# Routed expert blocks: transposes gathered behind one down product, expert numbers loaded earlier

## The chip, the cores and the metric

The kernel runs on one core of a Trainium2 chip. The metric is the device time of one execution in microseconds (us), median of several runs. The engines are TensorE (PE; PEld is its weight load), VectorE (DVE), ScalarE (ACT), GpSimd (POOL) and SyncE (SP, which issues most transfers).

## The reference

A cross-attention layer and a mixture-of-experts layer, each added to its input. The changed part is the second layer on 2048 tokens of 512 values, with 7 routed experts of which each token uses 2, and one shared expert:

```python
x = x + xattn(layernorm(x), ctx)
t = layernorm(x)                                    # 2048 x 512
gate = t @ Wr + br                                  # 7 experts, the best 2 are taken
probs = softmax(gate of the chosen 2)
u = t @ Wup[e] + bup[e]                             # 512 x 512 each
g = silu(u @ Wgate[e] + bgate[e]) * u
eo = g @ Wdown[e] + bdown[e]
x = x + sum over e of probs * eo  +  shared expert(t)
```

## The kernel before

The program has five stages on the same core: projections, attention, `output` (attention's output product, routing, the shared expert for the first half of the tokens), `routed` (the experts) and `late` (the shared expert for the second half, and the sum of all). Each stage ends at a barrier of all engines.

`output` gives each (token, expert) pair a row in `xs_dram`, in order of experts, each expert's rows filled up to a multiple of 128. `routed` then works through N = `NBLK` = 38 blocks of 128 such rows; `blk_k` holds the expert of each block (1 to 7) and `blk_w` the place of its weights. All weights are kept as a high and a low 16-bit part in `w_exp`, 7 places of one expert each; POOL loads and splits the experts from the third one on while blocks run (L192, L202 to L210). A product of a block with a 512 x 512 weight is 12 matmuls of 512 columns: 4 chunks of the contraction, for each high x high, low x high and high x low (`product`, L1907).

A block n goes through this chain:

- x: PE turns the block's rows, four 128 x 128 transposes (`transposes`, L1897, into `psX`); ACT copies out the high part `e_xT` (`hi_part`, L1834), DVE makes the low part (`lo_part`, L1862).
- u: PE's up product into `psU`; DVE scales and adds the bias (`biased`, L1865) into `e_u`; PE turns it (into `psUT`); ACT and DVE make the two parts of `e_uT`.
- g: PE's gate product into `psG`; DVE adds the bias (`e_g`), ACT takes silu (L1855), DVE multiplies by `e_u` (L1889); PE turns the result (into `psGT`); ACT and DVE make the two parts of `e_gT`.
- y: PE's down product into `psY`; ACT scales it out (`e_y`, L1848); SP stores it.

PSUM tiles `psX`, `psU`, `psUT` and `psG` are parts of one allocation, shown as `quad` in rows; `e_uT` has one buffer, `e_xT` and `e_gT` have two. The blocks are pipelined by hand: in `step(n)`, each engine does its parts of blocks n+1 (x), n (u and gate), n-1 (turning g) and n-2 (down), in the order in which the code stands; engines meet through semaphores alone. PE's order in a step is: up product of n; first half of the down product of n-2 (6 matmuls); turn g of n-1; turn u of n; second half of the down product; turn x of n+1; gate product of n. `run` writes out 4 steps, then a loop of 8 rounds with 4 steps each, then the last steps. The expert of a block is read from `blk_k` and `blk_w` into registers of PE by `value_load` (TENSOR_LOAD in an order of instructions): two loads ahead of each up product and one ahead of each down product. The addresses of the weights are set in registers between matmuls (ISA and REGISTER_ALU).

Of the kernel before, what the change touches and what calls it, by code (L numbers as in the profile page):

```python
# [21 lines left out]
F32 = mybir.dt.float32  # L22
# [36 lines left out]
UNROLL = 4  # L59
E_EARLY = 2  # L60
# [30 lines left out]
def build(nc, t, out, upto=99, dbg=None):  # L91
# [17 lines left out]
    with ctx:  # L109
# [13 lines left out]
        late_sb = Map(nc, SBUF_LO + 2 * PER_E, SBUF_LO + 3 * PER_E)  # L123
# [17 lines left out]
        blk_w = const("blk_w", [P, NBLK], I32)  # L141
# [45 lines left out]

        def load_half(eng, raw, loaded, k, half, m):

            shared = isinstance(k, int) and k in (0, E + 1)  # L190
            src = s_dram[m][:, ds(half * 2, 2), :] if shared else w_dram[m][:, ds((k - 1) * KD + half * 2, 2), :]
            eng.dma_start(raw, src).then_inc(loaded, 16)  # L192

        def split_half(pool, raw, loaded, arrived, k, half, m, n, piece):

            x = (k % E if isinstance(k, int) else k) * 2 + half
            hi, lo = (w_exp[:, ds(x, 1), m, y, :, :].rearrange("p o k n -> p (o k n)") for y in range(2))
            w = raw.rearrange("p k n -> p (k n)")
            ws = ws_tile[:, :].broadcast_to([P, KD // 2 * D])
            if piece == 0:  # L200
                pool.wait_ge(loaded, 16 * arrived)
                pool.tensor_tensor(hi, w, ws, ALU.mult).then_inc(w_scaled, 1)  # L202
            elif piece == 1:
                pool.wait_ge(w_scaled, 2 * n + 1)

                pool.tensor_tensor(seen[:, :], ws_tile[:, :], ws_tile[:, :], ALU.add)
                pool.tensor_scalar(w, w, WS, 0.0, ALU.mult, ALU.add).then_inc(w_scaled, 1)  # L207
            else:
                pool.wait_ge(w_scaled, 2 * n + 2)
                pool.tensor_tensor(lo, w, hi, ALU.subtract).then_inc(split_done, 1)  # L210

        def scale_half(act, raw, loaded, arrived, k, half, m, n, piece):

            hi = w_exp[:, k % E * 2 + half, m, 0, :, :]
# [1005 lines left out]
def output(nc, t, sem, g_):  # L1220

    w_exp, ident, oT_all, wo, slot, prob, pmat, blk_k, blk_w, b_up, b_gate = (
        g_[k] for k in "w_exp ident oT_all wo slot prob pmat blk_k blk_w b_up b_gate".split())
# [32 lines left out]
    wrap = low("wrap", [P, NBLK], F32)  # L1256
# [43 lines left out]
    with ExitStack() as ps:  # L1300
# [139 lines left out]
        def _(dve):  # L1440
# [174 lines left out]
        def _(pe):  # L1615
# [38 lines left out]
            def weight(m, y, q):  # L1654
                return w_exp[:, q // 2, m, y, q % 2, :]
# [61 lines left out]
def routed(nc, t, sem, g_):  # L1717

    w_exp, blk_k, blk_w, ident, seen, ws_tile, bias = (
        g_[k] for k in "w_exp blk_k blk_w ident seen ws_tile bias".split())  # L1720
# [22 lines left out]
    def run(eng, step):  # L1743

        peeled = 4
        left = (N - 2 - peeled) % UNROLL
        for n in range(peeled):
            step(n, n % 2, n // 2)
        if N - 2 - peeled >= UNROLL:
            with eng.Fori(0, (N - 2 - peeled) // UNROLL) as r:  # L1750
                for q in range(UNROLL):
                    step(r * UNROLL + peeled + q, q % 2, r * (UNROLL // 2) + (peeled + q) // 2)
        for n in range(N - 2 - left, N - 2):
            step(n, n % 2, n // 2)
        for n in range(N - 2, N + 2):
            step(n, n % 2, n // 2)

    with ExitStack() as ps:  # L1758
# [73 lines left out]
        def _(act):  # L1832
# [27 lines left out]
        def _(dve):  # L1860
# [6 lines left out]
            def step(n, j, i):  # L1867
                if live(n, 0):
                    dve.wait_ge(s["u_mm"], n + 1)
                    dve.wait_ge(s["b_up"], (n + 1) * 16)  # L1870
                    at_least(dve, s["g_r"], n - 1)
                    at_least(dve, s["uT_t"], n - 1)
                    biased(u[:, j], psU, 0, s["u_r"], n)
                if live(n, 1):
                    dve.wait_ge(s["gT_h"], n)
                    lo_part(gT[:, (j + 1) % 2], psGT).then_inc(s["gT_l"], 1)
                if live(n, 0):
                    dve.wait_ge(s["uT_h"], n + 1)
                    lo_part(uT, psUT).then_inc(s["uT_l"], 1)
# [14 lines left out]
        def _(pe):  # L1894
# [16 lines left out]
            def turn(n):  # L1911
                return pe.value_load(blk_k[0:1, ds(n, 1)], min_val=0, max_val=E)

            def place(n):
                return pe.value_load(blk_w[0:1, ds(n, 1)], min_val=0, max_val=E - 1)

            def step(n, j, i):
                if live(n, 0):
                    k, w = turn(n), place(n)
                    pe.wait_ge(g_["split_done"], k * (2 * NM) + 2 * NM + 1)  # L1920
                    pe.wait_ge(s["xT_l"], n + 1)
                    at_least(pe, s["u_r"], n)
                    product(psU, xT[:, j], w, 0).then_inc(s["u_mm"], 1)
                if live(n, 2):
                    w2 = place(n - 2)
                    pe.wait_ge(s["gT_l"], n - 1)
                    at_least(pe, s["y_r"], n - 2)
                    product(psY, gT[:, j], w2, 2, range(0, KD // 2))
# [18 lines left out]
            step(-1, 1, -1)  # L1947
            run(pe, step)
# [5 lines left out]
            for c, dst in enumerate((psX, psU)[:UP_EARLY]):  # L1954
                terms = [(q, x, y) for q in range(KD) for x, y in ((0, 0), (1, 0), (0, 1))]
                for i, (q, x, y) in enumerate(terms):
                    ins = pe.matmul(dst[:, :], w_exp[:, 2 + q // 2, 0, y, q % 2, c * P:(c + 1) * P], g_["xT_late"][:, 0, q, x, :],
# [4 lines left out]
def late(nc, t, sem, g_, out):  # L1962
# [28 lines left out]
    def yr(m, k):  # L1991
        return yr0[:, m, k, :] if m < 6 else yr1[:, m - 6, k, :]
# [4 lines left out]
    with ExitStack() as ps:  # L1997
# [167 lines left out]
        def _(pe):  # L2165
# [7 lines left out]
            def weight(m, y, q):  # L2173
                return w_exp[:, 2 + q // 2, m, y, q % 2, :]
# [80 lines left out]
```

## Time and profile before

| | |
|---|---|
| runs | 1024.02 us median of 3 (1016.83 to 1025.42) |
| profiled execution, first to last instruction | 1015.6 us |
| fastest run less that span | 1.2 us |
| PE busy in it | 918.0 us (90%) |
| stage `routed` | from 570 to 948 us of the span |
| PE busy from 570 to 945 us | 361.00 of 375.00 us |

The profile has no time of its own beside its span. Busy time of PE counts a matmul longer than the step from one matmul to the next, because matmuls overlap: a row of 12 begins its successor some 2.6 us after its own begin, though 2.76 us busy. So the text reads starts of rows, not busy times.

### The profile page before, as it was taken

What the parts mean: (1) busy time and instruction counts of PE and PEld (TensorE: products, weight loads), DVE (VectorE), ACT (ScalarE), POOL (GpSimd) and SP (SyncE); (2) the same over time, 40 slices, a digit from 0 to 9 for tenths busy, and PEclk for the clock granted to TensorE, in tenths of its full rate; (3) what the DMA queues carried; (4) which work ended last, traced back from release to release, by engine and by line L of the source; (5) the groups of instructions that cost most, each with busy time, mean ns of one, the idle gap of its engine ahead of it and who ended that gap; (6) DMA issues with size and microseconds to landing.
All of it is one profiled execution on the core that took longest, in us unless ns stands there. A gap on an engine that the chain in (4) does not pass through costs nothing. (4 is left out here: it accounts for less than half of the span.)

```text
span 1015.6 us, 17154 instructions
## 1 busy us (share of the span) xinstructions
PE 918.0 (90%) x5077; PEld 403.7 (40%) x5078; DVE 641.9 (63%) x1026; ACT 463.2 (46%) x846; POOL 618.7 (61%) x565
## 2 busy tenths in 40 slices
PE   3799886799989899989999599999999999999998
PEld 1354443122212122246644244454454554554443
DVE  7787777698878788367765154444444544443388
ACT  3365555688878787623351032332332332322440
POOL 5465446377777684543147589998899999000372
PEclk9899998699999999999999799999999999999999
DMA  8134435445455432143427646565555565335666
GB/s 279 32 110 141 138 105 150 135 166 176 157 174 174 149 103 66 44 126 137 174 103 278 210 166 187 167 206 168 183 189 181 188 202 163 110 124 188 220 192 232
DMA packets 104521, 162.31 MB, mean 160 GB/s; under 512 B 10904, under 2 KB 53912, under 8 KB 104080
## 3 DMA queue, kind: packets, MB, share of 16 engines
q1 hardware_dynamic: 91520, 116.45, 35.0%
q0 software_dynamic: 12896, 45.10, 13.4%
q8 instruction: 30, 0.49, 0.2%
q14 instruction: 27, 0.22, 0.1%
q10 hardware_dynamic: 48, 0.05, 0.0%
HBM read 108.08 MB, written 53.48 MB: 159 GB/s over the span
## 5 line engine op out<-in xcount | busy, mean ns | idle before, releaser
L1013 ACT ACTIVATE p_t<-a_psT 128x512 f32<-128x512 f32 x256 | 138.9, 595 | 47.7 <-PE a_psT L1136 46.4
L1060 DVE TENSOR_REDUCE nm<-quad 128x4 bf16<-128x1984 f32 x60 | 133.9, 2232 | 35.8 <-PE quad L1121 35.8
L1907 PE MATMUL quad<-w_exp,e_xT 128*128 x456 | 106.8, 385 | 7.8 <-issue 4.0
L963 POOL TENSOR_TENSOR p_sum<-p_t,p_t 128x512 f32<-128x512 f32 x64 | 81.1, 1277 | 50.1 <-ACT p_t L1013 49.8
L1907 PE MATMUL e_psY<-w_exp,e_gT 128*128 x456 | 110.7, 379 | 0.9 <-ACT e_y L1848 0.9
L1907 PE MATMUL quad<-w_exp,e_uT 128*128 x456 | 104.9, 380 | 2.5 <-DVE e_uT L1862 2.5
L1136 PE MATMUL a_psT<-q_stk,k_stk 98*128 98x512 f16 x256 | 84.9, 402 | 14.1 <-ACT p_t L1013 8.8
L210 POOL TENSOR_TENSOR w_exp<-e_raw,w_exp 128x1024 f32 (+1 forms) x42 | 91.5, 2180 | 6.0 <-POOL e_raw L207 4.5
L202 POOL TENSOR_TENSOR w_exp<-e_raw,ws_tile 128x1024 f32 (+1 forms) x42 | 80.2, 1910 | 5.1 <-DMA e_raw<-in_L_ffn_Wup_dram 4.2
L1834 ACT ACTIVATE e_gT<-e_psGT 128x512 f16<-128x512 f32 x38 | 22.7, 597 | 124.0 <-PE e_psGT L1897 124.0
L1855 ACT ACTIVATE e_g<-e_g 128x512 f32<-128x512 f32 x38 | 23.9, 630 | 107.1 <-DVE e_g L1865 107.1
L1907 PEld LDWEIGHTS quad<-w_exp,e_xT 128*128 128x128 f16 x456 | 42.0, 99 | 72.2 <-issue 28.4
L1143 PE MATMUL a_psO<-p_t,v_all 128*32 128x512 f32 x512 | 67.0, 620 | 0.0
L1907 PEld LDWEIGHTS quad<-w_exp,e_uT 128*128 128x128 f16 x456 | 41.5, 98 | 54.6 <-issue 9.9
L1907 PEld LDWEIGHTS e_psY<-w_exp,e_gT 128*128 128x128 f16 x456 | 44.5, 98 | 46.6 <-issue 1.4
L1862 DVE TENSOR_TENSOR e_gT<-e_psGT,e_gT 128x512 f16<-128x512 f32 x38 | 26.3, 692 | 54.5 <-ACT e_gT L1834 54.5
L1865 DVE SCALAR_TENSOR_TENSOR e_g<-quad,bias 128x512 f32<-128x512 f32 x38 | 26.3, 692 | 53.0 <-PE quad L1907 53.0
L1889 DVE TENSOR_TENSOR e_g<-e_g,e_u 128x512 f32<-128x512 f32 x38 | 40.5, 1066 | 26.4 <-ACT e_g L1855 26.4
L1382 POOL DMA_INDIRECT xs_dram<-xn,slot x32 | 31.7, 991 | 40.3 <-DVE slot L1562 30.2
L1136 PEld LDWEIGHTS a_psT<-q_stk,k_stk 98*128 98x128 f16 x256 | 17.9, 97 | 95.4 <-issue 55.2
L1862 DVE TENSOR_TENSOR e_xT<-quad,e_xT 128x512 f16<-128x512 f32 x38 | 26.3, 691 | 42.2 <-ACT e_xT L1834 42.2
L2037 POOL MEMSET low<- 24x1 f32 x1 | 0.1, 88 | 83.8 <-POOLq L1758 83.8
(333 smaller groups left out, 1855.0 us busy)
## 6 DMA issues: line engine op xcount, KB each, us to landing
xs_dram<-zero SPq DMA_DIRECT2D x38, 256.0 KB, 7.2
e_x<-xs_dram SPq DMA_DIRECT2D x38, 256.0 KB, 4.0
bias<-in_L_ffn_bup_dram SPq DMA_DIRECT2D x38, 256.0 KB, 3.7
bias<-in_L_ffn_bgate_dram SPq DMA_DIRECT2D x38, 256.0 KB, 3.7
ys_dram<-e_y SPq DMA_DIRECT2D x38, 256.0 KB, 3.8
q_dram<-q_st SPq DMA_DIRECT2D x24, 256.0 KB, 2.8
k_dram<-k_st SPq DMA_DIRECT2D x24, 256.0 KB, 3.7
q_stk<-q_dram SPq DMA_DIRECT2D x64, 96.0 KB
```

Source lines behind the costliest of these rows:

```text
L202: pool.tensor_tensor(hi, w, ws, ALU.mult).then_inc(w_scaled, 1)
L210: pool.tensor_tensor(lo, w, hi, ALU.subtract).then_inc(split_done, 1)
L963: pool.tensor_tensor(p_sum[:, w % SUMS, :], probs(w, 0), probs(w, 1), ALU.add).then_inc(s["sum_1"], 1)
L1013: act.activation(probs(w, k), psT[:, k % 2], ACT.Exp, scale=SCALE / (QS * QS)).then_inc(s["exp"], 1)
L1060: dve.tensor_reduce(nm[:, i, :, 0:1].rearrange("p h o -> p (h o)"), psS[:, :, 0:NMAIN], AX.X, ALU.max, negate=True)
L1136: pe.matmul(psT[:, k % 2], k_stk[0:KR, w % SLOTS, k * P:(k + 1) * P], q_stk[0:KR, w % SLOTS, :], start=True, stop=True).then_inc(s["t_mm"], 1)
L1143: ins = pe.matmul(dst[j * HD:(j + 1) * HD, :], stationary(n), moving(n), start=first, stop=last, tile_position=(0, j * HD))
L1382: pool.indirect_dma_start(g_["xs_dram"], bass.IndirectOffsetOnAxis(ap=slot[:, k, n:n + 1], axis=0), xn2[:, n, :], None).then_inc(landed, 16)
L1862: return dve.tensor_tensor(pair[:, 1], src[:, :].rearrange("p (k n) -> p k n", n=P), pair[:, 0], ALU.subtract)
L1865: return dve.scalar_tensor_tensor(dst, src[:, :], 1.0 / WS, bias[:, m, :], ALU.mult, ALU.add).then_inc(done, 1)
L1889: dve.tensor_tensor(g[:, :], g[:, :], u[:, j], ALU.mult).then_inc(s["g_r"], 1)
L1907: ins = pe.matmul(dst[:, :], stationary, moving, start=(k == 0 and chunks[0] == 0), stop=(k == len(terms) - 1 and chunks[-1] == KD - 1))
```

## The change

On PE, a step now runs: the whole down product of n-2 (12 matmuls), turn u of n, turn g of n-1, turn x of n+1, gate product of n, up product of n+1. Around the cycle of steps the products stay in the same order (gate, up, down); the second half of the down product moves ahead of the transposes, and u is turned ahead of g. ACT and DVE make the parts of `e_uT` ahead of those of `e_gT`. Only `blk_k` is loaded, and each load serves the up, gate and down product of its block as far as the code of one round reaches: 7 loads in a round of four steps where there were 12. The load for the next up product stands behind the transposes of x, ahead of the gate product. `blk_w` is gone, and with it the three DVE instructions in `output` that made it. The weights of expert k now lie at place k-1; those of the shared expert lie at place 1 in `output` and at place 0 in `late`, whose tables are laid out to match.

```diff
+        def place_of(k):
+            return {0: 1, E + 1: 0}.get(k, k - 1) if isinstance(k, int) else k - 1
...
-            link(dve.tensor_scalar(wrap[:, :], blk_f[:, :], float(E), None, ALU.is_ge))
-            link(dve.scalar_tensor_tensor(wrap[:, :], wrap[:, :], -float(E), blk_f[:, :], ALU.mult, ALU.add))
             link(dve.tensor_copy(blk_k[:, :], blk_f[:, :]))
-            link(dve.tensor_copy(blk_w[:, :], wrap[:, :]))
...
@@ -1834,14 +1833,14 @@
             def step(n, j, i):
+                if live(n, 0):
+                    act.wait_ge(s["uT_t"], n + 1)
+                    at_least(act, s["g_mm"], n)
+                    hi_part(uT[:, 0], psUT).then_inc(s["uT_h"], 1)
                 if live(n, 1):
                     act.wait_ge(s["gT_t"], n)
                     at_least(act, s["y_mm"], n - 2)
                     hi_part(gT[:, (j + 1) % 2, 0], psGT).then_inc(s["gT_h"], 1)
-                if live(n, 0):
-                    act.wait_ge(s["uT_t"], n + 1)
-                    at_least(act, s["g_mm"], n)
-                    hi_part(uT[:, 0], psUT).then_inc(s["uT_h"], 1)
...
@@ -1871,12 +1870,12 @@
+                if live(n, 0):
+                    dve.wait_ge(s["uT_h"], n + 1)
+                    lo_part(uT, psUT).then_inc(s["uT_l"], 1)
                 if live(n, 1):
                     dve.wait_ge(s["gT_h"], n)
                     lo_part(gT[:, (j + 1) % 2], psGT).then_inc(s["gT_l"], 1)
-                if live(n, 0):
-                    dve.wait_ge(s["uT_h"], n + 1)
-                    lo_part(uT, psUT).then_inc(s["uT_l"], 1)
...
@@ -1908,44 +1907,56 @@
...
-            def step(n, j, i):
-                if live(n, 0):
-                    k, w = turn(n), place(n)
-                    pe.wait_ge(g_["split_done"], k * (2 * NM) + 2 * NM + 1)
-                    pe.wait_ge(s["xT_l"], n + 1)
-                    at_least(pe, s["u_r"], n)
-                    product(psU, xT[:, j], w, 0).then_inc(s["u_mm"], 1)
+            expert_of = {}
+            def expert(n, at):
+                if at not in expert_of:
+                    expert_of[at] = pe.value_load(blk_k[0:1, ds(n, 1)], min_val=1, max_val=E)
+                return expert_of[at]
+            def step(n, at, i):
+                j = at % 2
                 if live(n, 2):
-                    w2 = place(n - 2)
+                    w2 = expert(n - 2, at - 2) - 1
                     pe.wait_ge(s["gT_l"], n - 1)
                     at_least(pe, s["y_r"], n - 2)
-                    product(psY, gT[:, j], w2, 2, range(0, KD // 2))
+                    product(psY, gT[:, j], w2, 2).then_inc(s["y_mm"], 1)
+                if live(n, 0):
+                    pe.wait_ge(s["u_r"], n + 1)
+                    at_least(pe, s["uT_l"], n)
+                    transposes(psUT, u[:, j], s["uT_t"])
                 if live(n, 1):
                     pe.wait_ge(s["g_r"], n)
                     at_least(pe, s["gT_l"], n - 1)
                     transposes(psGT, g, s["gT_t"])
                 if live(n, 0):
-                    pe.wait_ge(s["u_r"], n + 1)
-                    at_least(pe, s["uT_l"], n)
-                    transposes(psUT, u[:, j], s["uT_t"])
-                if live(n, 2):
-                    product(psY, gT[:, j], w2, 2, range(KD // 2, KD)).then_inc(s["y_mm"], 1)
+                    w = expert(n, at) - 1
                 if live(n, -1):
                     pe.wait_ge(x_ld[(j + 1) % 2], (i + 1 if j == 0 else i + 2) * 16)
                     at_least(pe, s["xT_l"], n + 1)
                     transposes(psX, x_in[:, (j + 1) % 2], s["xT_t"])
+                    after = expert(n + 1, at + 1)
                 if live(n, 0):
                     pe.wait_ge(s["uT_l"], n + 1)
                     at_least(pe, s["g_in"], n)
                     product(psG, uT, w, 1).then_inc(s["g_mm"], 1)
+                if live(n, -1):
+                    pe.wait_ge(g_["split_done"], after * (2 * NM) + 2 * NM + 1)
+                    pe.wait_ge(s["xT_l"], n + 2)
+                    at_least(pe, s["u_r"], n + 1)
+                    product(psU, xT[:, (j + 1) % 2], after - 1, 0).then_inc(s["u_mm"], 1)
...
-    low = Map(nc, SBUF_LO, SBUF_LO + g_["PER_E"])
-    yr0 = low("l_yr0", [P, 6, TOP, D], F32)
-    yr1 = sb("l_yr1", [P, NT - 6, TOP, D], F32)
+    rows_back = sb("l_rows_back", [P, NT, TOP, D], F32)
```

PE, a step in the loop, before: from the end of the first half of the down product (`e_psY`) over the transposes (`ident` with `e_g`, `e_u`, `e_x`) to the gate product (`e_uT`).

```order
L1907 MATMUL e_psY<-w_exp,e_gT 128x512
L1897 MATMUL e_psGT<-ident,e_g 128x128 [waits e_gT_l,e_g_r]
...
L1897 MATMUL quad<-ident,e_u 128x128 [waits e_uT_l,e_u_r]
...
L1907 MATMUL e_psY<-w_exp,e_gT 128x512 x2
...
L1897 MATMUL quad<-ident,e_x 128x128 [waits e_xT_l,e_x_loaded0]
...
L1907 ISA [waits e_g_in,e_uT_l]
L1907 MATMUL quad<-w_exp,e_uT 128x512 x2
```

The same place now.

```order
L1906 MATMUL e_psY<-w_exp,e_gT 128x512
L1896 MATMUL quad<-ident,e_u 128x128 [waits e_uT_l,e_u_r]
...
L1896 MATMUL e_psGT<-ident,e_g 128x128 [waits e_gT_l,e_g_r]
...
L1896 MATMUL quad<-ident,e_x 128x128 [waits e_xT_l,e_x_loaded0]
...
L1915 TENSOR_LOAD blk_k
...
L1906 ISA [waits e_g_in,e_uT_l]
L1906 MATMUL quad<-w_exp,e_uT 128x512 x2
```

Between turning u and the gate product's wait for `e_uT_l` stood 6 matmuls and 4 transposes; now there are 8 transposes and one load.

PE, between the gate product and the next up product (`e_xT`), before.

```order
L1907 MATMUL quad<-w_exp,e_uT 128x512
L1912 ISA
L1912 TENSOR_LOAD blk_k
L1912 ISA x2
L1915 REGISTER_ALU
L1915 TENSOR_LOAD blk_w
L1915 ISA x2
L1920 ISA
L1921 REGISTER_ALU [waits w_split_done]
L1907 ISA [waits e_u_r,e_xT_l]
L1907 MATMUL quad<-w_exp,e_xT 128x512 x2
```

The same place now.

```order
L1906 MATMUL quad<-w_exp,e_uT 128x512
L1945 ISA
L1946 REGISTER_ALU [waits w_split_done]
L1906 ISA [waits e_u_r,e_xT_l]
L1906 MATMUL quad<-w_exp,e_xT 128x512 x2
```

Both loads are gone from there; the waits stay.

ACT, a step in the loop, before.

```order
L1834 ACTIVATE e_gT<-e_psGT 128x512 [waits e_y_mm,e_gT_t]
L1834 ACTIVATE e_uT<-quad 128x512 [waits e_g_mm,e_uT_t]
L1848 ACTIVATE e_y<-e_psY 128x512 [waits e_y_stored1,e_y_mm]
L1850 REGISTER_ALU
L1834 ACTIVATE e_xT<-quad 128x512 [waits e_u_mm,e_xT_t]
L1855 ACTIVATE e_g<-e_g 128x512 [waits e_g_in]
```

The same place now.

```order
L1833 ACTIVATE e_uT<-quad 128x512 [waits e_g_mm,e_uT_t]
L1833 ACTIVATE e_gT<-e_psGT 128x512 [waits e_y_mm,e_gT_t]
L1847 ACTIVATE e_y<-e_psY 128x512 [waits e_y_stored1,e_y_mm]
L1849 REGISTER_ALU
L1833 ACTIVATE e_xT<-quad 128x512 [waits e_u_mm,e_xT_t]
L1854 ACTIVATE e_g<-e_g 128x512 [waits e_g_in]
```

`e_uT` has moved ahead of `e_gT`; the rest of the step stands as before.

## Rows read from the trace of the kernel before

**Rows 1.** Busy time by stage: PE, PEld, DVE, ACT, POOL, then clock, DMA share, GB/s.

```profile
570.00:945.00 375.00, 361.00 (x1833) 182.25 (x1834) 167.87 (x228) 106.75 (x190) 264.45 (x232) 0.99 0.52 172
```

**Rows 2.** Waits of PE from 598 to 933 us: total, times, longest.

```profile
PE quad L1907 <- issue: 4.0, 9, 0.6
```

**Rows 3.** PE's order of time in one step: start, us, instruction.

```profile
704.01 2.76 PE L1907 MATMUL quad<-w_exp,e_uT 128*128 x12
706.85 2.76 PE L1907 MATMUL quad<-w_exp,e_xT 128*128 x12
709.44 1.46 PE L1907 MATMUL e_psY<-w_exp,e_gT 128*128 x6
710.74 0.60 PE L1897 MATMUL e_psGT<-ident,e_g 128*128 128x128 f32 x4
711.18 0.60 PE L1897 MATMUL quad<-ident,e_u 128*128 128x128 f32 x4
711.61 1.46 PE L1907 MATMUL e_psY<-w_exp,e_gT 128*128 x6
712.91 0.60 PE L1897 MATMUL quad<-ident,e_x 128*128 128x128 f32 x4
713.44 0.39 PE L1907 MATMUL quad<-w_exp,e_uT 128*128 x1
```

**Rows 4.** PE's order of time where a round of the loop ends.

```profile
722.84 2.76 PE L1907 MATMUL quad<-w_exp,e_uT 128*128 x12
726.12 2.76 PE L1907 MATMUL quad<-w_exp,e_xT 128*128 x12 [0.52 <-issue]
```

**Rows 5.** PE's order of time in step 1, which has no down product.

```profile
586.94 0.66 PE L1897 MATMUL e_psGT<-ident,e_g 128*128 128x128 f32 x4 [1.09 <-DVE e_g L1889]
587.54 0.66 PE L1897 MATMUL quad<-ident,e_u 128*128 128x128 f32 x4
...
589.69 2.54 PE L1907 MATMUL quad<-w_exp,e_uT 128*128 x11 [1.06 <-DVE e_uT L1862]
```

**Rows 6.** PE's order of time in the last steps.

```profile
932.79 2.76 PE L1907 MATMUL quad<-w_exp,e_uT 128*128 x12 [0.37 <-DVE e_uT L1862]
...
937.72 0.66 PE L1897 MATMUL e_psGT<-ident,e_g 128*128 128x128 f32 x4 [0.88 <-DVE e_g L1889]
...
940.57 2.76 PE L1907 MATMUL e_psY<-w_exp,e_gT 128*128 x12 [0.90 <-ACT e_y L1848]
```

**Rows 7.** ACT and DVE in the same step and the next one.

```profile
711.38 0.60 ACT L1834 ACTIVATE e_gT<-e_psGT 128x512 f16<-128x512 f32 x1 [3.21 <-PE e_psGT L1897]
711.87 0.59 ACT L1834 ACTIVATE e_uT<-quad 128x512 f16<-128x512 f32 x1
712.01 0.69 DVE L1862 TENSOR_TENSOR e_gT<-e_psGT,e_gT 128x512 f16<-128x512 f32 x1 [1.37 <-ACT e_gT L1834]
712.61 0.68 DVE L1862 TENSOR_TENSOR e_uT<-quad,e_uT 128x512 f16<-128x512 f32 x1
...
717.62 1.90 DVE L1889 TENSOR_TENSOR e_g<-e_g,e_u 128x512 f32<-128x512 f32 x1 [0.70 <-ACT e_g L1855]
...
719.45 0.68 DVE L1865 SCALAR_TENSOR_TENSOR e_u<-quad,bias 128x512 f32<-128x512 f32 x1
```

**Rows 8.** PE's order of time in step 0.

```profile
578.16 0.67 PE L1897 MATMUL quad<-ident,e_u 128*128 128x128 f32 x4 [0.79 <-DVE e_u L1865]
...
580.32 2.76 PE L1907 MATMUL quad<-w_exp,e_uT 128*128 x12 [1.06 <-DVE e_uT L1862]
```

**Rows 9.** DVE's order of time in `output`: first and last instruction for `blk_w`.

```profile
534.38 0.32 DVE L1586 TENSOR_SCALAR wrap<-blk_f 128x38 f32<-128x38 f32 x1
...
535.18 0.18 DVE L1589 CAST blk_w<-wrap 128x38 int32<-128x38 f32 x1
```

**Rows 10.** Busy time and clock of short stretches (columns as Rows 1).

```profile
572.70:577.40 4.70, 4.66 (x12) 1.58 (x12) 0.00 (x0) 0.00 (x0) 3.47 (x4) 0.59 0.83 281
...
585.70:589.60 3.90, 1.84 (x13) 1.27 (x12) 3.12 (x5) 1.68 (x3) 3.73 (x4) 1.00 0.59 180
589.60:600.00 10.40, 10.31 (x54) 5.32 (x55) 4.25 (x7) 2.80 (x5) 9.30 (x10) 1.00 0.48 175
```

More of the change, by code:

```diff
@@ L59 @@
 UNROLL = 4
+PEELED = 4
 E_EARLY = 2
@@ L122, in build @@
         w_exp = nc.alloc_sbuf_tensor_at("w_exp", [P, 2 * E, NM, 2, KD // 2, D], F16, offset=SBUF_LO)
-        late_sb = Map(nc, SBUF_LO + 2 * PER_E, SBUF_LO + 3 * PER_E)
+        late_sb = Map(nc, SBUF_LO + PER_E, SBUF_LO + 2 * PER_E)
         xT_late = late_sb("xT_late", [P, B // 2, KD, 2, S], F16)
@@ L140, in build @@
         blk_k = const("blk_k", [P, NBLK], I32)
-        blk_w = const("blk_w", [P, NBLK], I32)
         ws_tile = const("ws_tile", [P, 1], F32)
@@ L194, in split_half @@
         def split_half(pool, raw, loaded, arrived, k, half, m, n, piece):
-            x = (k % E if isinstance(k, int) else k) * 2 + half
+            x = place_of(k) * 2 + half
             hi, lo = (w_exp[:, ds(x, 1), m, y, :, :].rearrange("p o k n -> p (o k n)") for y in range(2))
@@ L212, in scale_half @@
         def scale_half(act, raw, loaded, arrived, k, half, m, n, piece):
-            hi = w_exp[:, k % E * 2 + half, m, 0, :, :]
+            hi = w_exp[:, place_of(k) * 2 + half, m, 0, :, :]
             if piece == 0:
@@ L1220, in output @@
 def output(nc, t, sem, g_):
-    w_exp, ident, oT_all, wo, slot, prob, pmat, blk_k, blk_w, b_up, b_gate = (
-        g_[k] for k in "w_exp ident oT_all wo slot prob pmat blk_k blk_w b_up b_gate".split())
+    w_exp, ident, oT_all, wo, slot, prob, pmat, blk_k, b_up, b_gate = (
+        g_[k] for k in "w_exp ident oT_all wo slot prob pmat blk_k b_up b_gate".split())
     low = Map(nc, SBUF_LO + E_EARLY * g_["PER_E"], g_["O_AT"])
@@ L1255, in output @@
     blk_f = low("blk_f", [P, NBLK], F32)
-    wrap = low("wrap", [P, NBLK], F32)
     mid = Map(nc, g_["O_AT"], g_["V_AT"])
@@ L1654, in weight @@
             def weight(m, y, q):
-                return w_exp[:, q // 2, m, y, q % 2, :]
+                return w_exp[:, 2 + q // 2, m, y, q % 2, :]
             def product(dst, terms):
@@ L1717, in routed @@
 def routed(nc, t, sem, g_):
-    w_exp, blk_k, blk_w, ident, seen, ws_tile, bias = (
-        g_[k] for k in "w_exp blk_k blk_w ident seen ws_tile bias".split())
+    w_exp, blk_k, ident, seen, ws_tile, bias = (
+        g_[k] for k in "w_exp blk_k ident seen ws_tile bias".split())
     tag = "e_"
@@ L1743, in run @@
     def run(eng, step):
-        peeled = 4
-        left = (N - 2 - peeled) % UNROLL
-        for n in range(peeled):
+        left = (N - 2 - PEELED) % UNROLL
+        for n in range(PEELED):
             step(n, n % 2, n // 2)
-        if N - 2 - peeled >= UNROLL:
-            with eng.Fori(0, (N - 2 - peeled) // UNROLL) as r:
+        if N - 2 - PEELED >= UNROLL:
+            with eng.Fori(0, (N - 2 - PEELED) // UNROLL) as r:
                 for q in range(UNROLL):
-                    step(r * UNROLL + peeled + q, q % 2, r * (UNROLL // 2) + (peeled + q) // 2)
+                    step(r * UNROLL + PEELED + q, q % 2, r * (UNROLL // 2) + (PEELED + q) // 2)
         for n in range(N - 2 - left, N - 2):
@@ L1946, in step @@
                     product(psG, uT, w, 1).then_inc(s["g_mm"], 1)
-            step(-1, 1, -1)
-            run(pe, step)
+                if live(n, -1):
[3 more added lines that the diff above has]
+                    product(psU, xT[:, (j + 1) % 2], after - 1, 0).then_inc(s["u_mm"], 1)
+            rounds = (N - 2 - PEELED) // UNROLL
+            for n in range(-1, PEELED):
+                step(n, n, n // 2)
+            expert_of.clear()
+            with pe.Fori(0, rounds) as r:
+                for q in range(UNROLL):
+                    step(r * UNROLL + PEELED + q, q, r * (UNROLL // 2) + (PEELED + q) // 2)
+            expert_of.clear()
+            for n in range(PEELED + rounds * UNROLL, N + 2):
+                step(n, n, n // 2)
             pe.wait_ge(late_ld, 32)
@@ L1956, in _ @@
                 for i, (q, x, y) in enumerate(terms):
-                    ins = pe.matmul(dst[:, :], w_exp[:, 2 + q // 2, 0, y, q % 2, c * P:(c + 1) * P], g_["xT_late"][:, 0, q, x, :],
+                    ins = pe.matmul(dst[:, :], w_exp[:, q // 2, 0, y, q % 2, c * P:(c + 1) * P], g_["xT_late"][:, 0, q, x, :],
                                     start=(i == 0), stop=(i == len(terms) - 1))
@@ L1991, in yr @@
     def yr(m, k):
-        return yr0[:, m, k, :] if m < 6 else yr1[:, m - 6, k, :]
+        return rows_back[:, m, k, :]
     def row(m):
@@ L2173, in weight @@
             def weight(m, y, q):
-                return w_exp[:, 2 + q // 2, m, y, q % 2, :]
+                return w_exp[:, q // 2, m, y, q % 2, :]
             def product(dst, terms):
```

4 lines of the change are left out of this document (removed).

## The prediction, made before the changed kernel ran

> **What bounds the kernel now.** I read the busy times by stage first. The stage `routed` takes more than a third of the span, and PE is busy in 361 of 375 us there at a granted clock of 0.99 [rows 1], so PE's row of instructions sets the pace. The view of waits adds that PE waited for hardly anything the profile can name: 4.0 us of "issue" in 9 pieces, and no wait for POOL's weights [rows 2]. That total understates the gaps, since a matmul's modelled end lies after the start of the next one. I therefore went to the order of time and took the distances between starts.
>
> One step, from gate product to gate product, is 9.43 us [rows 3]. The up product's 12 matmuls take 709.44 - 706.85 = 2.59 us, and each half of the down product 1.30. Four transposes take 0.43 to 0.44. So the bare work of a step is 3 x 2.59 + 3 x 0.435 = 9.08 us. The other 0.35 lies in two places: 0.25 between gate and up product (706.85 - 704.01 - 2.59), where the two loads of the expert stand, and 0.10 between turning x and the gate product (713.44 - 712.91 - 0.43). Once in four steps, where a round of the loop ends, the first gap is 726.12 - 722.84 - 2.59 = 0.69 [rows 4]. From the gate product of step 1 to that of step 37 there are 36 steps in 932.79 - 589.69 = 343.10 us [rows 5, 6], 9.53 each.
>
> The second gap is the end of a chain through three engines. PE turns u; ACT and DVE make the two parts of `e_uT`; then the gate product may start. In the step shown it ends at 712.61 + 0.68 = 713.29 on DVE, and the gate product starts 0.15 later [rows 3, 7]. From the start of turning u to the gate product it is 713.44 - 711.18 = 2.26 us. The kernel before fills this time with the second half of the down product and the turning of x: 0.43 + 1.30 + 0.43 = 2.16. The chain is just covered.
>
> **The gap before the up product goes.** Both loads leave it. Of the single load that stands before the down product, no trace can be seen: up starts at 706.85, down at 709.44, exactly 12 matmuls later [rows 3]. A load fits under one product, and two do not. In the new order at most one load stands between products (before the down product, in the first two steps of a round), and the others stand behind transposes. I cost them at nothing; what hides them is the product, or the wait below, that PE is working through. At the end of a round the jump and one load now follow two products instead of one; the jump's own price is 0.69 - 0.25 = 0.44 us, so the bound for 8 rounds is 0 to 3.5 us. I take 0, because one load behind one product showed nothing. If only this part had been made, a step would be 9.08 + 0.10 and the gain some 12 us.
>
> **The cover of the chain goes too.** Ahead of the gate product PE now has, from the start of turning u, only twelve transposes: 3 x 0.435 = 1.30 us. The chain itself gets a little shorter, since ACT and DVE take u first. By the rows of g, which now stands where u will stand: start of turning to start of ACT 711.38 - 710.74 = 0.64, ACT to DVE 712.01 - 711.38 = 0.63 [rows 3, 7]; then DVE's 0.68 for `e_uT` and 0.15 to the gate product. That is 2.10 us. There are two places in the kernel before that already run in the new arrangement. In step 1, where no down product exists yet, turning u at 587.54 is followed by turning x alone, and the gate product starts at 589.69: 2.15 us, with g ahead in ACT and DVE, and the profile books 1.06 us of idle PE on `e_uT` [rows 5]. In step 0 it is 580.32 - 578.16 = 2.16 us, with nothing ahead, and 1.06 idle again [rows 8]. So the chain lies between 2.10 and 2.16; I take 2.10, from the steady step. PE will stand idle for about 2.10 - 1.30 = 0.8 us in every step.
>
> A step becomes three products and the chain: 3 x 2.59 + 2.10 = 9.87 us against 9.53, or +0.34 x 36 = +12.2 us. With 2.16 it is +14.4.
>
> **What else is late or early.** The up product's result must reach PE through DVE before u can be turned; the whole down product, 2.59 us, now covers that. Even in the step where DVE's multiplication took 1.90 us, `e_u` was ready at 719.45 + 0.68 = 720.13 [rows 7], and in the new order u would be turned three products after 713.44, at 721.2. ACT does `e_uT`, `e_gT`, `e_y` and `e_xT` at a pitch of 0.5, so DVE's part of `e_xT` ends some 3.5 us after the start of turning u; the up product that needs it starts 2.10 + 2.59 = 4.7 after. Stores and loads of SP hang on events that all come at the same places of the step or earlier, and its transfers have a step's time to land. In step 0 the turning of u of block 1 waits for DVE as before, so that step keeps its length but for 0.05. At the end, before, the last down product started 940.57 - 932.79 = 7.78 after the last gate product [rows 6]. Now the last turning of g comes at 2 x 2.59 = 5.2 after it (5 are needed for g: 937.72 - 932.79 = 4.93), and a chain of 2.1 follows: 7.3, a gain of 0.5. In `output`, the three DVE instructions that made `blk_w` span 535.18 + 0.18 - 534.38 less one that stays, some 0.8 us [rows 9]; PE has the down products of the first half ahead of what waits for DVE there, so I count 0, at most 0.8. The weights' new places change no wait: POOL loads the same experts in the same order. `late` keeps all its instructions.
>
> **Sum.** +12.2 for 36 steps, -0.5 at the end, 0 to 3.5 at the ends of rounds (0 taken): +11.7 us on the profiled execution, 1015.6 to about 1027.3 us of span. That execution is like the fastest run (1016.83, 1.2 above the span); the median of the runs is 1024.02. On the median the forecast is 1035.7, say 1036 us, slower by 1.15%. Its own bounds are +11.7 (chain 2.10, no edges) and +17.4 (chain 2.16, edges 3.5): 1036 to 1041 on the median, and 1028 where the runs fall like the fastest one before.
>
> **Rivals.** *The transposes cover the chain after all.* If the gate product followed the transposes at once, a step would fall to 9.08, 36 x 0.45 = 16 us less: 1008 us. For it speaks that 0.35 us a step of gaps do go. Against it stand the two places with 1.06 us of idle [rows 5, 8] and the chain's own links. It decides at a chain of 9.53 - 7.77 = 1.76 us; below that the change is no loss. 7%.
>
> *The chain is shorter than its rows, near that point.* ACT and DVE would have to start on u before all four transposes are through, by 0.2 us or so; nothing in the rows does that. Half the loss: 1030 us. 9%.
>
> *Loads are not hidden.* PE now reads the expert behind the transposes and ahead of the gate product's wait. If that reading came only after them and pushed the gate product back by the 0.25 that two loads cost before, it would add 36 x 0.25 = 9 us, and the ends of rounds 3.5: 1048 us. Against it: the idle 0.8 us has room for it. 8%.
>
> *The clock falls.* Each step would have 2.10 us in which PE only turns or stands. When PE had been idle before its first product, 12 matmuls took 4.66 us at a mean granted clock of 0.59, in part at the lower level of 1.2 GHz [rows 10]; once a step, that costs 4.66 - 2.76 = 1.9, 36 times 68 us: 1104 us. But between the up product's end and the gate product of step 1, 3.9 us with nothing but transposes and idle, the granted clock was 1.00, and it was 1.00 after [rows 10]. 2%.
>
> The Trainium skill, "TensorE: Matmul & The Clock Gate", Part 4 (PE-mode transpose), says that transposes do not count as activity for the clock in the way that matmuls do; by that rule the new run of twelve transposes and the idle behind it would be one stretch without credit, and the rival above would decide. The clock of 1.00 through step 1 speaks against it at this length.
>
> **How the numbers follow.** The forecast holds 74%. A difference of about 1% is what a measurement of this kernel can tell from none, as the three runs lie 0.8% apart; the forecast's +11.7 us and more is just above that, so I give it 0.56 for slower by over 1% and 0.18 for within. Slower: 0.56 + 0.08 + 0.02 = 0.66. Within 1%: 0.18 + 0.09 = 0.27. Faster: 0.07. The range from 1027 to 1043 us holds the forecast with its bounds, runs like the fastest one, and the half loss.
>
> **What would show it.** In the profile of the changed kernel the waits of PE should name `e_uT` on DVE in nearly every step, about 0.6 us each as booked (2.10 less the start of turning x at 0.87 and its 0.60), some 23 us in all, where it was one wait of 0.37. Gate to gate should be 9.87 us in every step, without the longer fourth one; up product 2.59 after the gate product; turning u to gate product 2.10. I am wrong if that last distance is near 1.3 to 1.8, or if gaps between products remain.

## The result, and the profile after

The changed kernel takes 1029.37 us (median of 4 runs, 1027.36 to 1034.02), the kernel before 1021.86 (4 runs beside them, 1016.83 to 1025.42). The ratio is 1.0101, with a 95% interval from 1.0058 to 1.0144: slower by about 1%. The profiled execution has a span of 1027.0 us; 1027.3 was forecast.

The stage `routed` shows it first. PE is busy for less time in the same 375 us, at the same granted clock; the columns are those of [rows 1].

```profile
570.00:945.00 375.00, 346.39 (x1784) 179.06 (x1783) 174.37 (x224) 100.01 (x186) 265.37 (x232) 0.99 0.51 165
```

The waits of PE from 598 to 945 us (total, times, longest) were hardly any before [rows 2]. Now there is one in every step, and it names `e_uT`:

```profile
PE quad L1906 <- DVE e_uT L1861: 22.9, 35, 0.7
```

PE's order of time in one step of the changed kernel (start, us, instruction), to be laid beside [rows 3]:

```profile
707.46 2.76 PE L1906 MATMUL quad<-w_exp,e_uT 128*128 x12 [0.63 <-DVE e_uT L1861]
710.06 2.75 PE L1906 MATMUL quad<-w_exp,e_xT 128*128 x12
712.65 2.75 PE L1906 MATMUL e_psY<-w_exp,e_gT 128*128 x12
715.24 0.60 PE L1896 MATMUL quad<-ident,e_u 128*128 128x128 f32 x4
715.68 0.60 PE L1896 MATMUL e_psGT<-ident,e_g 128*128 128x128 f32 x4
716.12 0.60 PE L1896 MATMUL quad<-ident,e_x 128*128 128x128 f32 x4
717.34 1.03 PE L1906 MATMUL quad<-w_exp,e_uT 128*128 x4 [0.62 <-DVE e_uT L1861]
```

The gap between gate and up product is gone (710.06 - 707.46 = 2.60), and up to down takes 2.59. From turning u to the next gate product it is 717.34 - 715.24 = 2.10 us, of which the transposes fill 1.30. Gate to gate is 9.88 us.

ACT and DVE in the same step show the links of those 2.10 us (compare [rows 7]):

```profile
711.65 2.11 DVE L1888 TENSOR_TENSOR e_g<-e_g,e_u 128x512 f32<-128x512 f32 x1 [0.69 <-ACT e_g L1854]
713.69 0.68 DVE L1864 SCALAR_TENSOR_TENSOR e_u<-quad,bias 128x512 f32<-128x512 f32 x1
715.88 0.60 ACT L1833 ACTIVATE e_uT<-quad 128x512 f16<-128x512 f32 x1 [4.26 <-PE quad L1896]
716.51 0.69 DVE L1861 TENSOR_TENSOR e_uT<-quad,e_uT 128x512 f16<-128x512 f32 x1 [2.15 <-ACT e_uT L1833]
```

From turning to ACT 0.64, ACT to DVE 0.63, DVE 0.69, and 0.14 to PE. `e_u` itself is ready at 713.69 + 0.68 = 714.37, 0.87 us before PE turns it, though the multiplication ahead of it took 2.11.

The first step of each round is a little longer. The order of time of PE and ACT there (compare [rows 4]):

```profile
735.00 0.60 PE L1896 MATMUL quad<-ident,e_u 128*128 128x128 f32 x4
735.72 0.60 ACT L1833 ACTIVATE e_uT<-quad 128x512 f16<-128x512 f32 x1 [4.34 <-PE quad L1896]
737.22 0.60 PE L1906 MATMUL quad<-w_exp,e_uT 128*128 x2 [0.74 <-DVE e_uT L1861]
```

ACT starts 0.72 after turning began instead of 0.64, the chain is 2.22, and the step 9.99. This adds 0.11 a round, 0.9 us over 8 rounds. The jump's old 0.44 is no longer seen. The kernel before had the later start too: from turning x to the gate product it took 0.61 us in the first step of a round (732.79 - 732.18) where it was 0.53.

Three places at the ends answer to [rows 5, 6, 8]. First PE's order of time in steps 0 and 1:

```profile
580.28 2.76 PE L1906 MATMUL quad<-w_exp,e_uT 128*128 x12 [1.06 <-DVE e_uT L1861]
...
588.57 1.68 PE L1906 MATMUL quad<-w_exp,e_uT 128*128 x7 [0.63 <-DVE e_uT L1861]
```

And in the last steps, up to the first product of `late`:

```profile
945.25 2.76 PE L1906 MATMUL quad<-w_exp,e_uT 128*128 x12 [1.06 <-DVE e_uT L1861]
...
952.54 2.76 PE L1906 MATMUL e_psY<-w_exp,e_gT 128*128 x12 [1.50 <-DVE e_gT L1861]
955.13 1.24 PE L1968 MATMUL quad<-xT_late,w_exp 128*128 128x512 f16 x5
```

Step 0 takes 588.57 - 580.28 = 8.29 us where it was 589.69 - 580.32 = 9.37. The 36 steps behind it take 945.25 - 588.57 = 356.68 where it was 343.10. From the last gate product to the last down product it is 7.29 instead of 7.78. So -1.08 + 13.58 - 0.49 = +12.0 us lie in `routed`; the span grew by 11.4, since `late` behind it came out 0.6 shorter.

### The profile page after: what moved, and what is told of

It is laid out like the page before. It is cut to its first block and busy times, and to the rows that moved or that the text cites. A ratio compares the mean times of both kernels' runs of the same rounds, so it can differ in the third digit from the quotient of the medians.

```text
span 1027.0 us, 16980 instructions
## 1 busy us (share of the span) xinstructions
PE 916.7 (89%) x5077; PEld 406.5 (40%) x5078; DVE 650.2 (63%) x1023; ACT 458.9 (45%) x846; POOL 618.6 (60%) x565
## 5 line engine op out<-in xcount | busy, mean ns | idle before, releaser
L1906 PE MATMUL e_psY<-w_exp,e_gT 128*128 x456 | 104.7, 379 | 1.5 <-DVE e_gT L1861 1.5
L1833 ACT ACTIVATE e_uT<-quad 128x512 f16<-128x512 f32 x38 | 22.7, 597 | 164.1 <-PE quad L1896 164.1
L1861 DVE TENSOR_TENSOR e_uT<-quad,e_uT 128x512 f16<-128x512 f32 x38 | 26.3, 691 | 92.9 <-ACT e_uT L1833 92.9
L1906 PEld LDWEIGHTS quad<-w_exp,e_xT 128*128 128x128 f16 x456 | 45.0, 99 | 57.2 <-issue 4.7
L1888 DVE TENSOR_TENSOR e_g<-e_g,e_u 128x512 f32<-128x512 f32 x38 | 50.7, 1335 | 26.4 <-ACT e_g L1854 26.4
L211 POOL TENSOR_SCALAR e_raw<-e_raw 128x1024 f32<-128x1024 f32 x42 | 44.6, 1061 | 3.2
```

The lines of the kernel that those rows point to most:

```text
L1888: dve.tensor_tensor(g[:, :], g[:, :], u[:, j], ALU.mult).then_inc(s["g_r"], 1)
L1906: ins = pe.matmul(dst[:, :], stationary, moving, start=(k == 0 and chunks[0] == 0), stop=(k == len(terms) - 1 and chunks[-1] == KD - 1))
```

## The experiments

Theory: the two loads cost 0.25 us a step and their removal gives it back; turning u starts a chain of 2.10 us, and what PE has to do in that time decides the step. The rivals were that the loads in their new places still cost PE time, that the run of transposes itself is what PE pays for, and that the clock makes the difference. "Gate 1 to gate 37" below is the distance between the starts of these gate products, 36 steps; it was 343.10 before and 356.68 after. The kernel before ran beside the experiments too: 11 runs with a median of 1021.43 us for e1 to e4, 11 with 1019.43 for e5 to e8. Spans that were expected are worked out from the 1027 us of the changed kernel's profile, and several were missed, because the place of step 1's gate product moves between executions: 588.57 us in the changed kernel, 592.57 in e7, 593.34 in e1, 593.48 in e3, though what is edited there acts in later steps or, in e7, is covered by the wait. So the distance from gate 1 to gate 37 is what tells the theories apart.

**e1_split_six.** The changed kernel with half of the down product put back, between turning g and turning x:

```diff
-                    product(psY, gT[:, j], w2, 2).then_inc(s["y_mm"], 1)
+                    product(psY, gT[:, j], w2, 2, range(0, 2))
...
                     transposes(psGT, g, s["gT_t"])
+                if live(n, 2):
+                    product(psY, gT[:, j], w2, 2, range(2, KD)).then_inc(s["y_mm"], 1)
```

Expected: 

> The changed kernel with 6 of the 12 matmuls of the down product put back between turning g and turning x. Theory (uncovered chain): from turning u to the gate product there are then 0.43 + 0.43 + 1.30 + 0.43 = 2.6 us of work against a chain of 2.10, the wait for e_uT goes, a step is 9.08 us, 36 steps are 29 us shorter than in the changed kernel, span about 999 us (16 below the kernel before). Rival (the loss comes from the loads or from the order of ACT and DVE): step stays near 9.88, span 1027. Rival (an interrupted product itself costs time): step between 9.3 and 9.6, span 1008 to 1018.

Measured: 1010.77 us (6 runs), ratio to the kernel before 0.990 [0.9875, 0.9926]; gate 1 to gate 37 in 333.30 us. PE's order of time in a typical step:

```profile
886.86 1.46 PE L1906 MATMUL e_psY<-w_exp,e_gT 128*128 x6
888.16 0.60 PE L1896 MATMUL quad<-ident,e_u 128*128 128x128 f32 x4
...
889.03 1.46 PE L1906 MATMUL e_psY<-w_exp,e_gT 128*128 x6
...
890.76 2.75 PE L1906 MATMUL quad<-w_exp,e_uT 128*128 x12
```

Turning u to gate product is now 2.60 us of work without a gap, no `e_uT` is waited for, and the step is the bare 9.08. That rules out the rival by which an interrupted product itself costs time, although the span of 1008.8 us lies in the range given for it and not at 999: 4.8 us of the difference lie ahead of step 1. But 333.30 over 36 is 9.26: some steps are longer, and the view of waits names another chain, for `e_u` ahead of turning u. The waits from 598 to 945 us:

```profile
PE quad L1896 <- DVE e_u L1864: 4.5, 6, 1.2
```

One such step, in order of time:

```profile
698.89 1.92 POOL L206 TENSOR_TENSOR w_exp<-e_raw,ws_tile 128x1024 f32 x1
698.99 2.38 DVE L1888 TENSOR_TENSOR e_g<-e_g,e_u 128x512 f32<-128x512 f32 x1 [0.70 <-ACT e_g L1854]
...
701.29 0.68 DVE L1864 SCALAR_TENSOR_TENSOR e_u<-quad,bias 128x512 f32<-128x512 f32 x1
...
702.03 0.66 PE L1896 MATMUL quad<-ident,e_u 128*128 128x128 f32 x4 [0.57 <-DVE e_u L1864]
```

The half product ahead of turning u covers the making of `e_u` for 1.30 us only. Where DVE's multiplication takes 2.4 us, that is not enough. So the down product has two gaps to fill, one on each side of turning u, and the change put all of it on one side.

**e2_split_three.** The same with a quarter put back (`range(0, 3)` ahead, `range(3, KD)` behind).

Expected: 

> The changed kernel with 3 of the 12 matmuls of the down product behind turning g. Theory: work from turning u to gate 1.30 + 0.65 = 1.95 us against a chain of 2.10, so 0.15 us of wait stays; a step is 7.78 - 0.65 + 2.10 = 9.23 us, span about 1004 us. Rival (something else than the cover of the chain makes the step long): 9.5 to 9.9, span 1014 to 1027.

Measured: 1008.86 us (4 runs), ratio 0.9885 [0.9847, 0.9922]; gate 1 to gate 37 in 335.85. A step in PE's order of time:

```profile
896.97 0.60 PE L1896 MATMUL quad<-ident,e_u 128*128 128x128 f32 x4
...
897.84 0.81 PE L1906 MATMUL e_psY<-w_exp,e_gT 128*128 x3
...
899.07 1.25 PE L1906 MATMUL quad<-w_exp,e_uT 128*128 x5
```

Turning u to gate product is 2.10 again: three matmuls (0.65) bring the cover to 1.95, the chain still ends last by 0.15, and the step is 9.23 = 9.08 + 0.15. The chain's length is the same at two amounts of cover, and the loss falls one for one with the cover. The waits for `e_u` are 1.0 us in 4. The span is 1008.4 where about 1004 was expected; 2.4 us of that lie ahead of step 1 (590.95 for 588.57), most of the rest in steps longer than the typical one. Between e1 and e2 the runs do not tell a difference.

**e3_loads_back.** The changed kernel with two fresh loads between gate and up product, and none behind the transposes of x:

```diff
-                    after = expert(n + 1, at + 1)
...
-                    pe.wait_ge(g_["split_done"], after * (2 * NM) + 2 * NM + 1)
+                    again = pe.value_load(blk_k[0:1, ds(n + 1, 1)], min_val=1, max_val=E)
+                    after = expert(n + 1, at + 1)
+                    pe.wait_ge(g_["split_done"], again * (2 * NM) + 2 * NM + 1)
```

Expected: 

> The changed kernel with two fresh loads of the expert's number between the gate product and the up product, as before; the load behind the transposes of x is gone. Theory (the loads opened the gap of 0.25 us): the gap is back, 0.25 us a step and 0.25 to 0.3 at the ends of rounds, which now fall elsewhere; 36 x 0.25 = 9 us, span about 1036 us. Rival (the gap came from the order of products or the wait on the weights, which are unchanged here): no gap, span 1027.

Measured: 1039.22 us (4 runs), ratio 1.0178 [1.0142, 1.0213]; gate 1 to gate 37 in 362.55, 5.87 more than the changed kernel, or 0.16 a step. The gap is back in PE's order of time, after gate's 2.6 us:

```profile
905.88 2.76 PE L1906 MATMUL quad<-w_exp,e_uT 128*128 x12 [0.74 <-DVE e_uT L1861]
908.64 2.76 PE L1906 MATMUL quad<-w_exp,e_xT 128*128 x12
```

In the steps of the loop it is 0.12 to 0.26 us wide and mostly under the 0.25 that was expected. Here both loads read one table and the place is worked out in a different way, so the old pair need not cost exactly this. That two loads between the gate and the up product cost PE time is shown. That the loads cost nothing in the changed kernel's places is shown by the typical steps of e1 and e8, which have them there and take the bare 9.08.

**e4_g_first.** The changed kernel with ACT and DVE back in the old order, the parts of `e_gT` ahead of those of `e_uT`; PE as changed:

```diff
+                if live(n, 1):
+                    act.wait_ge(s["gT_t"], n)
...
                 if live(n, 0):
                     act.wait_ge(s["uT_t"], n + 1)
...
-                if live(n, 1):
-                    act.wait_ge(s["gT_t"], n)
```

The same swap is made in DVE's code.

Expected: 

> The changed kernel with ACT and DVE making e_gT ahead of e_uT, while PE still turns u ahead of g. Theory (the chain through ACT and DVE sets the gate product): e_uT must wait until g, turned 0.43 later, is through ACT and DVE, chain 0.43 + 0.64 + 0.50 + 0.63 + 0.69 + 0.15 = about 3.0 us instead of 2.10; step 10.8, span about 1060 us. Rival (PE's own work sets the step): no change, span 1027.

Measured: 1072.92 us (1 run); gate 1 to gate 37 in 394.09. PE, ACT and DVE in order of time:

```profile
699.98 0.60 PE L1896 MATMUL quad<-ident,e_u 128*128 128x128 f32 x4
...
701.55 0.59 ACT L1833 ACTIVATE e_uT<-quad 128x512 f16<-128x512 f32 x1
...
702.29 0.68 DVE L1861 TENSOR_TENSOR e_uT<-quad,e_uT 128x512 f16<-128x512 f32 x1
...
703.12 1.68 PE L1906 MATMUL quad<-w_exp,e_uT 128*128 x7 [1.66 <-DVE e_uT L1861]
```

ACT takes u only 1.57 us after its turning began, the chain is 3.14 us, where about 3.0 was expected, and the step 10.91. The chain is 1.04 longer than in the changed kernel and the step 1.03: the transposes hide nothing more than their 1.30.

**e5_loads_alone.** The first half of the change without the second: the changed kernel's loads, places and code of a step, with the order of the kernel before on PE, ACT and DVE (the split of e1, g turned ahead of u, and e4's swap).

Expected: 

> The order of the kernel before on PE, ACT and DVE (half the down product, turn g, turn u, other half, turn x; g first on ACT and DVE), with the loads, the code of a step and the places of the changed kernel. Theory: the gap ahead of the up product goes and the chain stays just uncovered by 0.10, so a step is 9.08 + 0.10 = 9.18 us, 36 x 0.35 = 13 us less than before. From the gate product of step 1 to that of step 37 some 331 us (before 343.1). Rival (the loads were worth little and the new order made the gain of the split kernels): 9.4 to 9.5 a step, 338 to 342 us.

Measured: 1009.67 us (4 runs), ratio 0.9902 [0.9864, 0.994]; gate 1 to gate 37 in 334.90, 8.20 less than before. PE's order of time:

```profile
878.61 2.76 PE L1906 MATMUL quad<-w_exp,e_uT 128*128 x12
881.21 2.75 PE L1906 MATMUL quad<-w_exp,e_xT 128*128 x12
...
885.53 0.60 PE L1896 MATMUL quad<-ident,e_u 128*128 128x128 f32 x4
...
887.79 1.47 PE L1906 MATMUL quad<-w_exp,e_uT 128*128 x6
```

Gate to up is 2.60, turning u to gate 2.26 as before, the step 9.18 = 9.08 + 0.10. The distance is 334.90 where 331 was expected, a mean of 9.30 a step: the first step of a round takes about 0.1 more, four steps take 9.75 to 9.97, and a few others are up to 0.2 longer. In the longest, from the gate product at 728.84, DVE's multiplication took 2.90 us and PE waited for `e_g` ahead of turning g. The loads' half of the change is a gain of about 1%.

**e6_one_run_alone.** The second half without the first, and without the new order of ACT and DVE: the kernel before, with the whole down product ahead of the transposes.

```diff
-                    product(psY, gT[:, j], w2, 2, range(0, KD // 2))
+                    product(psY, gT[:, j], w2, 2).then_inc(s["y_mm"], 1)
...
-                if live(n, 2):
-                    product(psY, gT[:, j], w2, 2, range(KD // 2, KD)).then_inc(s["y_mm"], 1)
```

Expected: 

> The kernel before with only the down product in one run of twelve ahead of both transposes; loads, ACT and DVE as before. Theory: turning g, then the chain of u, 2.15 to 2.26 us, uncovered, and the gap of 0.25 to 0.69 stays: 7.78 + 0.435 + 2.2 + 0.36 = 10.8 us a step, 388 us from gate 1 to gate 37, 45 more than before. Rival (a product in one run costs PE nothing and the chain is not what is waited for): 9.53, 343 us.

Measured: 1069.15 us (1 run); gate 1 to gate 37 in 389.77, 46.67 more than before, 1.30 a step. That is the half product that no longer stands under the chain. PE's order of time shows the gap ahead of up (945.40 - 942.53 = 2.87) and the bare chain (953.28 - 951.02 = 2.26):

```profile
942.53 2.76 PE L1907 MATMUL quad<-w_exp,e_uT 128*128 x12 [1.22 <-DVE e_uT L1862]
945.40 2.76 PE L1907 MATMUL quad<-w_exp,e_xT 128*128 x12
...
951.02 0.60 PE L1897 MATMUL quad<-ident,e_u 128*128 128x128 f32 x4
953.28 1.03 PE L1907 MATMUL quad<-w_exp,e_uT 128*128 x4 [1.22 <-DVE e_uT L1862]
```

**e7_more_transposes.** The changed kernel, with the four transposes of x done twice (the second set writes the same values):

```diff
+                    for c in range(KD):
+                        pe.transpose(psX[:, c * P:(c + 1) * P], x_in[:, (j + 1) % 2][:, c * P:(c + 1) * P], ident[:, :])
                     transposes(psX, x_in[:, (j + 1) % 2], s["xT_t"])
```

Expected: 

> The changed kernel with the four transposes of x done twice, 0.43 us of PE more in each step. Theory (PE stands idle behind them until e_uT is there): they fit into the idle 0.63 us, step 9.88 as in the changed kernel, 356.7 us from gate 1 to gate 37. Rival (a run of transposes itself makes the step long): 10.3 a step, 372 us.

Measured: 1033.13 us (1 run), and gate 1 to gate 37 in 356.68, to the hundredth as without the extra work. PE's order of time, and then the waits from 598 to 945 us:

```profile
917.48 0.60 PE L1896 MATMUL quad<-ident,e_u 128*128 128x128 f32 x4
...
919.58 0.60 PE L1906 MATMUL quad<-w_exp,e_uT 128*128 x2 [0.19 <-DVE e_uT L1861]
```

```profile
PE quad L1906 <- DVE e_uT L1861: 7.6, 35, 0.3
```

Again 2.10 us, with 16 transposes in it instead of 12. The idle time was idle; transposes are not the price. The run's time is 3.8 us above the changed kernel's median, inside that kernel's own runs, and nothing of it lies in these 36 steps: in the profile, 4.0 of the 4.2 us more of span lie ahead of step 1.

**e8_g_turned_first.** Made from what e1 showed: the split of e1, and on PE g turned ahead of u, while ACT and DVE still take u first. Ahead of turning u there are then 1.30 + 0.43 us for `e_u`, behind it 0.43 + 1.30 + 0.43 for `e_uT`.

```diff
-                    product(psY, gT[:, j], w2, 2).then_inc(s["y_mm"], 1)
+                    product(psY, gT[:, j], w2, 2, range(0, 2))
+                if live(n, 1):
...
+                    transposes(psGT, g, s["gT_t"])
...
                     transposes(psUT, u[:, j], s["uT_t"])
-                if live(n, 1):
...
-                    transposes(psGT, g, s["gT_t"])
+                if live(n, 2):
+                    product(psY, gT[:, j], w2, 2, range(2, KD)).then_inc(s["y_mm"], 1)
```

Expected: 

> The changed kernel with half the down product behind the turning of u, and g turned ahead of u on PE; ACT and DVE still make e_uT first. Theory, now with the second side that the kernel with six matmuls put back showed (u must be ready when PE turns it): between up product and turning u lie 1.30 + 0.44 = 1.73 us instead of 1.30, so most of the 8 waits for e_u go; from turning u to gate 0.43 + 1.30 + 0.43 = 2.16 just covers the chain of 2.10 if ACT may take u at once, but ACT and DVE take u ahead of g while g is there first, which costs u nothing. Step 9.08 to 9.1, 327 to 330 us from gate 1 to gate 37 (333.3 with six put back), span 4 us below that kernel at the same clock. Rival (turning g first delays e_uT again): 9.2 to 9.3, 331 to 335 us.

Measured: 1005.43 us (6 runs), ratio 0.985 [0.9821, 0.9879], the lowest median of all, though its interval touches those of e1 and e2; against the changed kernel's 1.0101 that is 2.5% less. Gate 1 to gate 37 in 329.80. PE's order of time and the longest waits from 598 to 945 us:

```profile
892.12 0.60 PE L1896 MATMUL e_psGT<-ident,e_g 128*128 128x128 f32 x4
892.55 0.60 PE L1896 MATMUL quad<-ident,e_u 128*128 128x128 f32 x4
892.99 1.46 PE L1906 MATMUL e_psY<-w_exp,e_gT 128*128 x6
...
894.72 1.46 PE L1906 MATMUL quad<-w_exp,e_uT 128*128 x6
```

```profile
PE e_psGT L1896 <- DVE e_g L1888: 1.4, 2, 0.9
```

The step is 9.08, with 2.17 us of work over a chain of 2.10, and only 329.80 - 36 x 9.08 = 2.9 us over the bare work remain in 36 steps.

## Why the prediction was right

**Gap ahead of the up product.** It went, as forecast, in the changed kernel and alone in e5: 8.20 us from gate 1 to gate 37, where the prediction put some 12 for this part by itself. Typical steps of e5 have the forecast 9.18; the missing 4 us are in its longer steps, about 1 of them in the first steps of rounds and some 3 in the four long ones, where DVE's multiplication comes late.

**Cover of the chain.** The chain was put at 2.10 us and is 2.10, at covers of 1.30, 1.73 (e7) and 1.95 (e2); the step was put at 9.87 and is 9.88. That the whole down product covers the making of `e_u` came true as well: DVE's multiplication took up to 2.96 us, and the waits above name `e_uT` alone. The 0.6 us that the profile was to book against `e_uT` are 0.62 or 0.63, their sum 22.9 where 23 was forecast. e6 shows the same mechanism from the other side, and e4 that the new order in ACT and DVE kept the loss from being nearly three times as large (394.09 - 334.90 = 59.2 us in place of 21.8). The change is thus a gain of 8.2 us and a loss of 21.8 (334.90 to 356.68), and the second is not a price of the first: e8 has the gain without the loss. By typical steps alone the same two parts are some 12.6 (343.10 - 36 x 9.18) and 25.2 (36 x 0.70); the longer steps of e5 lower both.

**The terms at the edges** were mis-sized, and cancel; this is luck. The 36 steps were put at +12.2 and came to +13.58, mostly by the ends of rounds. There 0 was taken, with 0.44 a round as bound, and every step was to be alike; 0.11 a round came, from another link, ACT's start on u. Step 0: -0.05 was taken, -1.08 came. The text let turning u wait for DVE as before; the wait was there, but DVE's multiplication ahead of `e_u` took 1.14 us at 584.47 where it had taken 2.37 at 584.51. Each of the two ended about 0.55 us behind an instruction of POOL that was running when it began, as told in the last section. Step 0 of e5, with the order of the kernel before, takes 8.28 too, with a multiplication of 0.73. So the 1.08 goes with where POOL stood in its work, and no run shows that the change made it. `blk_w`, with 0 to 0.8 us, shows nothing: the first gate product starts at 580.28 and did at 580.32. The end: -0.5 taken, -0.49 measured. In sum +12.0 in `routed` against +11.7.

**From the profile to the runs.** 1036 was forecast for the median, with bounds of 1036 to 1041, and 1029.37 came; it lies in the wider range of 1027 to 1043, which was left for runs like the fastest one. The sum was made on the profiled execution (1015.6 of span, the fastest run shown) and its difference added to the median of three runs. Of the 6.3 us that are missing, 2.2 are the base: the median before came out as 1021.86, not 1024.02. The other 4.2 are the difference: profile against profile it is +11.4, median against median +7.5, with an interval (0.0058 to 0.0144 of 1021.86) of 5.9 to 14.7 that holds both. Executions with the same mean granted clock speak for the larger one: at 0.968 the kernel before took 1017.14, 1017.38 and 1019.25 us beside the experiments, the changed kernel 1028.63 and 1030.10.

**The rivals.** The clock did not fall: 0.99 in the stage, and the gate product behind each wait takes its 2.60 us to the next product. The Trainium skill, "TensorE: Matmul & The Clock Gate", Part 4 (PE-mode transpose), has it that transposes do not count as busy time as matmuls do; with 2.10 us of nothing but transposes and waiting in each step, these traces show no effect of that. Loads not hidden: the reading ahead of the gate product added nothing to the chain's 2.10. A shorter chain, or one that twelve transposes cover: none was seen.

## What to carry to other kernels

A piece of work between two transposes may be there as cover for a chain on other engines: before moving it, take the distance from the chain's first instruction to the one that waits for its end, and sum what the engine still has to do between them. Look at both sides of the place that starts the chain, since what waits for its input needs cover as well. And test two halves of a change apart: here one was worth 1%, the other cost 2%, and the profile after showed only their sum.

## What was not expected of the hardware

DVE's multiplication of two f32 tiles of 128x512 took between 0.69 and 2.96 us in the changed kernel, with a mean of 1327 ns (35 of them from 598 to 945 us); in e1's step above it began 0.10 us behind POOL's multiplication of 1.92 us and ended 0.56 behind that one's end. The trace of the changed kernel has this as a regularity. Of its 38 multiplications in `routed`, 16 took 0.69 us and 22 took 0.81 or more. Each of the 22 ended 0.53 to 0.56 us behind the end of one of POOL's instructions that split weights (`w_exp` or `e_raw`). POOL's last such instruction ends at 866.95; the nine multiplications behind it all took 0.69. The other nine traces show the same, 0.53 to 0.56 for every long one. The rows of POOL, ahead of the multiplication at 711.65 above, and of DVE after POOL's end:

```profile
711.29 1.91 POOL L206 TENSOR_TENSOR w_exp<-e_raw,ws_tile 128x1024 f32 x1
...
870.25 0.69 DVE L1888 TENSOR_TENSOR e_g<-e_g,e_u 128x512 f32<-128x512 f32 x1 [0.69 <-ACT e_g L1854]
```

So the waits for `e_u` and `e_g` in e1, e5 and e8 depend on where POOL stands in its work when the multiplication begins. The Trainium skill, "SBUF — State Buffer", SBUF: two separate sides, says that a VectorE instruction with two inputs in SBUF and a GpSimd instruction that reads SBUF exclude each other for a whole instruction. The rows fit that in the main; in three of the 22, however, the multiplication began up to 0.50 us ahead of the POOL instruction whose end it followed. Spans on POOL are rough, and no run here took POOL's work away: that the long multiplications go with POOL's work is shown, the mechanism is argued.

ACT's work on u starts 0.08 us later in the first step of a round (0.72 against 0.64). Its wait compares with a value from a register that is set there; that this is the cause was not tried.

The first gate product ran at a lower clock in five of the ten profiled executions (e1, e3, e4, e6, e8). In e1 its 12 matmuls took 4.41 us, where the changed kernel's took 2.76 at 580.28. The two rows in e1's profile, PE's order of time and the busy time and clock of a stretch (columns as [rows 1]):

```profile
583.24 4.41 PE L1906 MATMUL quad<-w_exp,e_uT 128*128 x12 [1.06 <-DVE e_uT L1861]
```

```profile
584.00:588.00 4.00, 4.00 (x14) 1.57 (x13) 0.31 (x1) 0.00 (x0) 3.65 (x5) 0.67 0.41 132
```

The granted clock there was 0.67, so part of the stretch lay at 1.2 GHz and not at 2.4. What decides this from execution to execution was not found; it is some of the scatter between runs, and a reason why distances behind step 1 are compared here.
